# A three-attention transformer pipeline: output transposes moved from TensorE to VectorE, one mask product for two blocks, biases moved to ScalarE, new places in the order table

## The reference

```python
xn = layernorm(x)
# A: grouped-query attention, 16 query heads of 8 channels, 4 key/value heads, biases bq, bk, bv
# M: multi-head latent attention, causal, 16 heads, keys and values from a latent of 64 channels, rope
h  = x + A(xn) + F(xn)
# F(xn): r = xn + M(rmsnorm(xn)); r + moe(rmsnorm(r)), 4 experts of 512 hidden channels, the best one a token
hn = layernorm(h)
# B: multi-query attention, 16 query heads, 1 key/value head, with biases
y  = h + B(hn) + swiglu_ffn(hn)        # int8 weights, hidden 384
# each attention: softmax(q k^T / sqrt(8)) v, then a product with Wo
```

## Time and profile before

| | before |
|---|---|
| median of 3 runs, us | 2810.91 (2808.42 to 2811.84) |
| the profiled execution, its own time, us | 2806.16 |
| its span, us | 2804.4 |
| PE, busy share of the span | 93% |
| DVE | 82% |
| ACT | 62% |
| POOL | 29% |

### The profile page before, as it was taken

The page is one execution under the profiler, slowest core; times in us unless marked ns, Lnnn a source line. Parts: engine busy times, 40 slices in busy tenths (PEclk is TensorE's granted clock), DMA queues, the critical chain, the costliest instruction groups (busy, mean ns, idle before and its releaser), DMA issues. The chain is left out here.

```text
span 2804.4 us, 120631 instructions
## 1 busy us (share of the span) xinstructions
PE 2618.0 (93%) x50864; PEld 1434.5 (51%) x50864; DVE 2303.3 (82%) x6003; ACT 1735.6 (62%) x3538; POOL 813.7 (29%) x1385
## 2 busy tenths in 40 slices
...
GB/s 99 7 129 32 79 75 32 125 25 109 54 59 91 26 137 29 90 74 43 106 25 131 36 82 72 32 125 25 110 53 66 83 27 136 28 96 67 39 67 6
DMA packets 168044, 191.23 MB, mean 68 GB/s; under 512 B 24614, under 2 KB 150736, under 8 KB 167504
## 3 DMA queue, kind: packets, MB, share of 16 engines
...
q0 software_dynamic: 4096, 8.40, 1.1%
...
## 5 line engine op out<-in xcount | busy, mean ns | idle before, releaser
L1217 ACT ACTIVATE probs<-bank 128x512 f32<-128x512 f32 x2688 | 1461.7, 598 | 667.5 <-PE bank L617 661.0
L972 DVE TENSOR_REDUCE mx<-bank 128x1 f32<-128x512 f32 x2048 | 1281.4, 681 | 65.2 <-PE bank L617 52.2
L977 DVE CUSTOM_DVE_ANT_0 bank<-bank,mask 128x128 f32<-128x128 f32 (+3 forms) x1024 | 478.5, 517 | 106.6 <-PE bank L617 100.4
L617 PE MATMUL bank<-kp_B,qp_B 72*32 72x512 bf16 x4096 | 442.9, 392 | 18.8 <-issue 9.4
L617 PE MATMUL bank<-qp_B,kp_B 74*32 74x512 bf16 x4096 | 415.4, 384 | 2.2 <-ACT probs L1217 1.6
L617 PE MATMUL bank<-qp_A,kp_A 74*32 74x512 bf16 x4096 | 408.2, 380 | 6.7 <-DVE mx L972 6.1
L617 PE MATMUL bank<-kp_A,qp_A 72*32 72x512 bf16 x4096 | 384.2, 381 | 14.8 <-DVE mx L972 7.5
L1362 POOL TENSOR_SCALAR nms<-mx 128x16 bf16<-128x16 f32 x192 | 39.8, 207 | 1043.2 <-DVE mx L977 510.2
L617 PE MATMUL bank<-kp_M,qp_M 72*32 72x128 bf16 (+3 forms) x4096 | 314.7, 311 | 28.2 <-DMA kp_M<-parts_k 20.4
L617 PE MATMUL bank<-qp_M,kp_M 74*32 74x512 bf16 (+3 forms) x4096 | 284.8, 302 | 20.3 <-DVE mx L972 15.2
L738 PE MATMUL pv<-probs,vv_B 128*32 128x512 f32 x2048 | 275.6, 596 | 1.2 <-ACT probs L1217 1.0
...
## 6 DMA issues: line engine op xcount, KB each, us to landing
...
qp_M<-parts_q SPq DMA_DIRECT2D x144, 128.0 KB
kp_M<-parts_k SPq DMA_DIRECT2D x144, 128.0 KB
qp_A<-parts_q SPq DMA_DIRECT2D x144, 128.0 KB
qp_B<-parts_q SPq DMA_DIRECT2D x144, 128.0 KB
...
kp_A<-parts_k SPq DMA_DIRECT2D x144, 32.0 KB
...
```

The lines of the kernel that those rows point to most:

```text
L617: ins = pe.matmul(dst[at:at + n], lhsT[:, at:at + n], rhs, start=start, stop=stop, tile_position=(0, at))
L972: v.tensor_reduce(mx[:, g % 2, at:at + 1], s1[BANK[a, g, u]][:], AX.X, ALU.max) \
L977: v.tensor_tensor_reduce(bank[:, 0:keys], bank[:, 0:keys], mask[:, SEQ - keys:SEQ], 1.0, LOWEST, ALU.add, ALU.max, mx[:, g % 2, at:at + 1] ...
L1217: act.activation(probs[:, slot, :], s2[BANK2[a, g, u]][:], ACT.Exp).then_inc(sig[f"{a}_exp"], 1)
```

## The change

- **Output transposes.** `out_copy`, `out_turn`'s transposes and `o_turn` leave PE and ACT. DVE gets `out_copy`, one transpose instruction over 128x512 f32 that turns each 32x32 block, from `pv` in PSUM to `osb` in SBUF; the reciprocal and the product now read `osb`; and `o_turn`, one more such instruction from `otok` to `oT`. The order of Wo's rows is changed on the host to fit. The banks that held the transposes are no longer taken.
- **Mask.** Where a unit of M holds two diagonal blocks, one mask product of 256 columns (the same 128 for both) stands in place of two of 128. Of the 64 masks a batch (each four products), 40 remain; the number of columns is the same.
- **Biases.** `full_q` and `full_k` of A and B are written by ACT. Two small instructions at the start of the program scale the biases for it.
- **Shifts.** One transfer writes both rows of maxima, 12 a batch in place of 24.
- **Latent.** `m_latn` (normalize) and `m_lat_turn` (scale the transposed) are two steps on DVE with places of their own.
- **Places.** `T` and `LATE` have new numbers throughout.

```diff
-         m_lat_turn=1.55, m_k=1.763, split_mk=1.85, m_v=1.95, turn_xn=2.283, a_q=2.542, split_aq=2.687, a_k=2.8,
...
+         m_lat=0.943, m_latn=1.53, m_lat_turn=1.55, m_k=1.724, split_mk=1.75, m_v=1.813, turn_xn=2.283, a_q=2.538,
...
-    "PE": dict(),
+    "PE": dict(m_v=-0.035, o_proj=-0.027, m_lat_turn=0.123, b_v=-0.027, ranks=-0.104, a_q=-0.077, turn=-0.047,
+               down=0.015, out_turn=0.036),
...
-        "out_turn": [(f"{a}_otok", g + 1)] if name == "out_turn" else [],
-        "o_turn": [(f"{a}_oT", 1)], "o_proj": [({"M": "x2_ready", "A": "gqa_added", "B": "y_ready"}.get(a), 1)],
+        "o_proj": [({"M": "x2_ready", "A": "gqa_added", "B": "y_ready"}.get(a), 1)],
...
-        otok = sb("otok", [P, TILES, D])
+        otok = sb("otok", [P, SEQ])
...
-                for s in range(2):
-                    sp.dma_start(qp[a][SHIFT + s:SHIFT + s + 1, GROUP * g:GROUP * g + GROUP, :],
-                                 nmT[16 * s:16 * s + 16, g % 2, :]).then_inc(sig[f"{a}_shift"], 16)
+                sp.dma_start(qp[a][SHIFT:ROWS2, GROUP * g:GROUP * g + GROUP, :], nmT[:, g % 2, :]) \
+                    .then_inc(sig[f"{a}_shift"], 16)
...
-                for hh, c, col, q in unit_parts(a, u):
+                for part, (hh, c, col, q) in enumerate(unit_parts(a, u)):
                     h = GROUP * g + hh
                     scores = s2[BANK2[a, g, u]][:, col:col + q]
                     ins = in_columns(scores, k_rows(a, h, ROWS2)[:, P * c:P * c + P], q_rows(a, h, ROWS2)[:, SEQ - q:SEQ],
-                                     True, a != "M")
-                    if a == "M":
-                        ins = in_columns(scores[:, 0:P], identb[:], late_keys[:], False, True)
+                                     part == 0, a != "M")
+                if a == "M":
+                    cols = [col for _, _, col, _ in unit_parts(a, u)]
+                    if len(cols) == 1:
+                        ins = in_columns(s2[BANK2[a, g, u]][:, 0:P], identb[:], late_keys[:], False, True)
+                    else:
+                        blocks = s2[BANK2[a, g, u]][:].rearrange("p (b n) -> p b n", n=P)[:, 0:cols[1] // P + 1:cols[1] // P]
+                        ins = in_columns(blocks, identb[:], late_keys[:].unsqueeze(1).broadcast_to([P, 2, P]), False, True)
                 ins.then_inc(sig[f"{a}_s2_ps"], 1)
...
-            def out_turn(b, a, g):
-                m = misc_bank(b, f"{a}_otok", g + 1)
-                pe.wait_ge(sig[f"{a}_osb"], total(b, f"{a}_osb", g + 1))
-                for t in range(TILES):
-                    ins = pe.transpose(m[:, P * t:P * t + P], osb[:, g % 2, P * t:P * t + P], ident[:])
-                ins.then_inc(sig[f"{a}_ot_ps"], 1)
-
-            def o_turn(b, a):
-                m = misc_bank(b, f"{a}_oT", 1)
-                pe.wait_ge(sig[f"{a}_otok"], total(b, f"{a}_otok"))
-                turns4(m, otok, f"{a}_oT_ps")
...
-            def m_lat_turn(b):
+            def m_latn(b):
                 v.wait_ge(sig["lat_rstd"], total(b, "lat_rstd"))
                 if not b.first:
                     v.wait_ge(sig["latT_ps"], total(b.prev, "latT_ps"))
                 normed(latn, lat, lmv, lsq[:, 1], "latn_ready")
+
+            def m_lat_turn(b):
                 v.wait_ge(sig["latT_ps"], total(b, "latT_ps"))
                 if not b.first:
...
-            def query(b, s, ps, bias):
-                v.wait_ge(sig[ps], total(b, ps, 1))
-                for s_last, value in last_user(b, turn_full, s[1], f"{s}_split", 4):
-                    v.wait_ge(s_last, value)
-                v.tensor_scalar(full[s[1]][:], misc[SPARE[f"{s}_full", 1]][:], vcol(bias), SCALE,
-                                       ALU.add, ALU.mult).then_inc(sig[f"{s}_full"], 1)
-
-            def key(b, s, ps, bias, n):
-                v.wait_ge(sig[ps], total(b, ps, 2))
-                for s_last, value in last_user(b, turn_full, s[1], f"{s}_split", 4):
-                    v.wait_ge(s_last, value)
-                v.tensor_scalar(full[s[1]][0:n, :], misc[SPARE[f"{s}_full", 1]][0:n, :], vcol(bias, n), None,
-                                       ALU.add).then_inc(sig[f"{s}_full"], 1)
...
+            def out_copy(b, a, g):
+                v.wait_ge(sig[f"{a}_pv"], total(b, f"{a}_pv", len(CLUSTERS[a]) * (2 * g + 2)))
+                for s_last, value in last_user(b, turn_osb, g % 2, f"{a}_otok", g + 1):
+                    v.wait_ge(s_last, value)
+                v.transpose(osb[:, g % 2, :], pv[0][:]).then_inc(sig[f"{a}_osb"], 1)
+
             def out_turn(b, a, g):
 
-                v.wait_ge(sig[f"{a}_ot_ps"], total(b, f"{a}_ot_ps", g + 1))
-                m = misc[SPARE[f"{a}_otok", g + 1]][:].rearrange("p (t h c) -> p t h c", t=TILES, c=VHALF)
-                r = rc[:, g % 2, :].rearrange("p (t h) -> p t h", t=TILES)
+                v.wait_ge(sig[f"{a}_osb"], total(b, f"{a}_osb", g + 1))
+                m = osb[:, g % 2, :].rearrange("p (k h c) -> p k h c", h=2, c=VHALF)
+                r = rc[:, g % 2, :].rearrange("p (k h) -> p k h", h=2)
                 v.reciprocal(r, m[:, :, :, HD]).then_inc(sig[f"{a}_rc"], 1)
                 v.wait_ge(sig[f"{a}_rc"], total(b, f"{a}_rc", g + 1))
                 if g == 0:
-                    for s_last, value in last_user(b, turn_otok, 0, f"{a}_oT_ps", 1):
+                    for s_last, value in last_user(b, turn_otok, 0, f"{a}_oT", 1):
                         v.wait_ge(s_last, value)
-                width = 2 * GROUP * HD
-                dst = otok[:, :, width * g:width * g + width].rearrange("p t (h d) -> p t h d", d=HD)
-                v.tensor_tensor(dst, m[:, :, :, 0:HD],
-                                r.unsqueeze(3).broadcast_to([P, TILES, 2 * GROUP, HD]), ALU.mult) \
-                                    .then_inc(sig[f"{a}_otok"], 1)
+                dst = otok[:].rearrange("p (k g h d) -> p k g h d", g=TWOS, h=2, d=HD)[:, :, g]
+                v.tensor_tensor(dst, m[:, :, :, 0:HD], r.unsqueeze(3).broadcast_to([P, SEQ // TILE, 2, HD]), ALU.mult) \
+                    .then_inc(sig[f"{a}_otok"], 1)
+
+            def o_turn(b, a):
+                v.wait_ge(sig[f"{a}_otok"], total(b, f"{a}_otok"))
+                for s_last, value in last_user(b, turn_oT, 0, f"{a}_o_ps", 1):
+                    v.wait_ge(s_last, value)
+                v.transpose(oT[:], otok[:]).then_inc(sig[f"{a}_oT"], 1)
...
-            def out_copy(b, a, g):
-                act.wait_ge(sig[f"{a}_pv"], total(b, f"{a}_pv", len(CLUSTERS[a]) * (2 * g + 2)))
-                for s_last, value in last_user(b, turn_osb, g % 2, f"{a}_ot_ps", g + 1):
-                    act.wait_ge(s_last, value)
-                act.activation(osb[:, g % 2, :], pv[0][:], ACT.Copy).then_inc(sig[f"{a}_osb"], 1)
-
-            def o_turn(b, a):
-                act.wait_ge(sig[f"{a}_oT_ps"], total(b, f"{a}_oT_ps"))
-                for s_last, value in last_user(b, turn_oT, 0, f"{a}_o_ps", 1):
-                    act.wait_ge(s_last, value)
-                act.activation(oT[:], misc[SPARE[f"{a}_oT", 1]][:], ACT.Copy).then_inc(sig[f"{a}_oT"], 1)
...
+            def query(b, s, ps, bias):
+                act.wait_ge(sig[ps], total(b, ps, 1))
+                for s_last, value in last_user(b, turn_full, s[1], f"{s}_split", 4):
+                    act.wait_ge(s_last, value)
+                act.activation(full[s[1]][:], misc[SPARE[f"{s}_full", 1]][:], ACT.Identity, bias=scaled_bias[:, bias:bias + 1],
+                               scale=SCALE).then_inc(sig[f"{s}_full"], 1)
+
+            def key(b, s, ps, bias, n):
+                act.wait_ge(sig[ps], total(b, ps, 2))
+                for s_last, value in last_user(b, turn_full, s[1], f"{s}_split", 4):
+                    act.wait_ge(s_last, value)
+                act.activation(full[s[1]][0:n, :], misc[SPARE[f"{s}_full", 1]][0:n, :], ACT.Identity,
+                               bias=vcol(bias, n)).then_inc(sig[f"{s}_full"], 1)
```

More of the change, by code:

```diff
@@ L116 @@
             "B": ((0, 4), (4, 8), (8, 12), (12, 16))}
-T = dict(x_load=-0.9, x_norm=-0.066, res0=1.148, x_scaled=0.46, turn_xr=0.9, m_q=1.107, split_mq=1.25, m_lat=0.995,
-         m_lat_turn=1.55, m_k=1.763, split_mk=1.85, m_v=1.95, turn_xn=2.283, a_q=2.542, split_aq=2.687, a_k=2.8,
-         a_v=3.432, split_ak=3.649, pack=0.319, pack_a=1.414,
-         nms=1.16, nmT=1.5, lag=1.986, pv_M=3.114, pv=3.265, out_copy=1.188, out_turn=0.125, o_turn=0.222, o_proj=0.382,
-         x2_norm=0.352, e0=13.6, x2_scaled=-0.691, turn_r2=-0.5, gate=-0.318, ranks=0.157, route=0.15, route_step=0.043, scatter=0.75, xp_in=1.58, xp_turn=2.314, weights=1.15, wgap=0.209, wnext=0.2, up=2.849, step=0.248, later=0.3,
-         y_out=0.25, gather=0.618, moe_added=1.272, down=0.03,
-         b0=0.12, x1_scaled=0.177, res1=0.75, turn_x1=0.513, b_q=0.801, split_bq=0.18, b_k=1.03, split_bk=0.195, b_v=1.248,
-         ff=1, ff_down=0.358)
@@ L129 @@
-LATE = {
-    "SP": dict(shift_turn=0.067),
-    "PE": dict(),
```

(25 more changed lines are left out.)

46 lines of the change are left out of this document (28 added, 18 removed).

## The result

The changed kernel takes 2773.55 us (median of 4 runs, 2769.78 to 2780.79) against 2809.66 for the kernel before: a ratio of 0.9875, interval 0.9858 to 0.9891. That is 1.25% faster where 2.0% was forecast, inside the range. The profiled execution took 2775.06 us.

The account below looks back on a forecast made before the run. PE was taken to bound M, PE and DVE together A and B. M's -2.2 and A and B's -1.3 us a batch made -56 us over 16, with -1.2 at the end: forecast 2754 us, 8-in-10 range 2675 to 2810.

Parts of the forecast that it names:

- M stretch, -2.2 us a batch: In M, limited by PE alone, removed PE transposes, idle time and mask cost save 2.2 us a batch.
- DVE's transposes, 0.65 us: Six new DVE transposes a batch in A and B take 0.65 us each, adding 3.9 us.
- The rival of two passes: Each DVE transpose takes two passes, 1.25 us, putting the run at about 2812 us; chance 0.11.
- DVE's biases, -2.96 us in A and B: DVE loses full_q and full_k of A and B, saving 2.96 us a batch in those stretches.
- DVE's waits for PE, -2.2 us: Of DVE's 6.0 us of waits in A and B, those at `res` (1.4) and `latT` (0.8) go.
- PE's wait for the latent, gone: PE's 20.1 us of waiting for `latn` in the run goes, or falls under 0.5 us a batch.
- a sign that the prediction named: The prediction called itself wrong if DVE's waits in A and B stayed at 6 us.
- New places, costed at nothing: Steps at new places cost nothing in the sum; one landing too late would cost 0.7 to 1.5 us.
- PE is the limit everywhere: Rival: all removed PE time counts, giving 2685 us, or 2652 with idle weight loads; chance 0.17.
- The idle weight loads: Weight loads of PE's `osb` transposes stand idle 33.7 us; left out of the sum, possible extra gain where PE limits.
- DVE's queue held by `pv`: Rival: ACT's 3.8 us a batch wait for PE's last probs_v moves into DVE's queue, giving 2851 us; chance 0.12.
- The end: At the run's end, two copies and two sets of transposes give way to two DVE transposes, saving 1.2 us.

Follow-up runs that it names:

- extra_m: The changed kernel with one more unread DVE transpose in front of each of B's two out_copy a batch, in the M stretch: 2779.77 us, ratio 0.9891.
- small_parts: The kernel before with only the merged mask, ACT biases, single shift transfer and split latent step, old numbers, transposes still on PE: 2806.59 us, ratio 0.9993.
- old_places: The changed kernel with the place numbers of the kernel before and no shifts of PE's order: 2874.59 us, ratio 1.0229 to the kernel before.
- pe_turns: The changed kernel, new numbers included, with output transposes back on PE and their copies on ACT: 2864.05 us, ratio 1.0200 to the kernel before.
- bias_back: The changed kernel with A's and B's biases back on DVE: 2779.34 us, ratio 0.9895 to the kernel before.
- extra_ab: The changed kernel with one more unread DVE transpose in front of each out_copy of M and A, in the A and B stretches: 2798.85 us, ratio 0.9949.
- both_moved: The changed kernel with x1's transposes two score units later and the latent normalized ahead of A's reciprocal, product and transpose on DVE: 2785.90 us, ratio 0.9901.
- warm_x1: The changed kernel with eight more unread PE transposes of the identity in front of PE's wait for x1: 2751.36 us, ratio 0.9765 to the kernel before.
- old_warm: The changed kernel with the old place numbers, plus sixteen PE transposes of the identity in front of PE's wait for the latent: 2843.11 us, ratio 1.0101.

## Why the prediction came out where it did

- **M stretch, -2.2 us a batch.** Right in size, -2.4 on average, and right in that DVE's transposes there are nearly free (extra_m). But PE's work off M is not worth 2.2 us by itself: on average the transposes alone take 0.5 us off M at the old places (small_parts to old_places) and 3.1 at the new ones (pe_turns to the changed kernel).
- **DVE's transposes, 0.65 us.** They take 0.71 and 0.70 on average, inside the bounds of 0.63 to 0.80. The rival of two passes, 1.25 us, is out. The Trainium skill, page "VectorE: DVE Perf Modes", section "The three transpose paths", gave the figure from which the estimate of 1.24 us was worked out, four times its 311 ns for 128x128 in bf16. The trace does not agree with that scaling for this f32 operation, and the measurement decides; the page's own figure no run here shows.
- **DVE's biases, -2.96 us in A and B.** This step failed. It set work in one piece of a stretch against work in another. The biases stood in A2 and B4, which PE limits, so taking them away gave 0.07%, within the interval of no change, with the mask and the shift besides (small_parts), and putting them back costs about 0.2% (bias_back). The transposes came into pieces that DVE fills, A1 and B1 above all, where about half of DVE's work shows (extra_ab).
- **DVE's waits for PE, -2.2 us; PE's wait for the latent, gone.** Wrong, and by a sign that the prediction named: DVE's waits in A and B stayed near 6 us (6.0 before, 5.7 after). `res` gave 0.8 of its 1.4 us, `latT` kept its 0.8. Net, A and B were to be 1.3 us shorter and are 0.8 longer on average. The wait for the latent grew from 20.1 to 24.7 us, since DVE's reciprocal, product and transpose now stand ahead of `latn`; that it can go and give nothing is shown by both_moved. And what PE gave up in A came back as its own idle time.
- **New places, costed at nothing.** This is the largest miss: they are worth 3.5% on the new steps. Without them the change would be 2.3% slower than before. That the time lies inside the range is luck. The sum has the biases and the mask at -49 us, the rest of the change with its waits at -8, the places at nothing: -57. The runs have -2 (small_parts), +66 (to old_places) and -99 (to the changed kernel), -35 in all. Two errors of 47 and 74 us one way met one of 99 the other.
- **PE is the limit everywhere.** Out as a whole: it gave 2685 or 2652 us. Its 94 us for the transposes are near what pe_turns lost (91), at the new places only; at the old ones the same step costs 66. What a step is worth goes by the piece that it is put in. The idle weight loads, 34 us and more, do not show on top of the 94: the loss was 91. The rule of the Trainium skill, page "TensorEngine Tiling (Array Packing)", section "Key Properties", that a change of tiling mode drains the array, was not tested by itself. In these runs no cost beyond the products' own shows, but pe_turns also takes 102 us of transposes off DVE, which could hide one.
- **DVE's queue held by `pv`.** DVE waited 33.5 us, 14.7 of them once; the rest is 1.2 us a batch, a little over the 1 us forecast and under the 3.5 from which it would decide.
- **The clock.** No step of the prediction had it. That it costs time here is shown by warm_x1 (the mean granted clock of its five runs is 0.976 to 0.978, that of the changed kernel's four 0.965 to 0.970), and in one piece by old_warm.
- **The end.** Of the 11 us that came off behind the last start of that `res`, 1.2 were forecast. small_parts has 4.6 of them (79.3 us against 83.9), without being faster as a whole; the cause of the rest stays open.
